# Row maxima of the first two heads of a group on 32-row tiles of the TensorE array

## The reference, cut to what matters

```python
# layer 0: 16 heads of 4 columns, layer 1: 16 heads of 8 columns; 512 queries, 512 keys, 2 sequences
scores = einsum('bhsk,bhtk->bhst', Q, K) / sqrt(hd)
attn   = softmax(scores, axis=-1)        # needs the largest score of every query row
out    = einsum('bhst,bhtv->bhsv', attn, V)
```

## Time and profile before

| | |
|---|---|
| time, median of 3 runs | 538.16 us (537.77 to 544.53) |
| time of the profiled execution | 538.86 us |
| its span | 537.1 us |
| granted TensorE clock, mean | 0.976 |
| PE busy | 481.1 us (90%) |
| DVE busy | 315.2 us (59%) |
| ACT busy | 278.7 us (52%) |
| main loop of layer 0 | about 137 to 250 us |
| main loop of layer 1 | about 327 to 449 us |

### The profile page before, as it was taken

The page is one execution under the profiler, slowest core; times in us unless marked ns, Lnnn a source line. Parts: engine busy times, 40 slices in busy tenths (PEclk is TensorE's granted clock), DMA queues, the critical chain, the costliest instruction groups (busy, mean ns, idle before and its releaser), DMA issues.

```text
span 537.1 us, 7612 instructions
## 1 busy us (share of the span) xinstructions
PE 481.1 (90%) x2782; PEld 313.7 (58%) x2782; DVE 315.2 (59%) x826; ACT 278.7 (52%) x414; POOL 136.3 (25%) x136
## 2 busy tenths in 40 slices
PE   5899799999889999999999988989999988879970
PEld 4678678887433443434997864334443434769970
DVE  4654544566787878764263576877888762402223
ACT  6635343553455666778454653556665664106540
POOL 5765713331631011210100000101111005422561
PEclk9999899999999999999999997999999999989995
DMA  8970200000610000020000000000000004430003
GB/s 315 316 237 2 77 2 0 1 0 2 237 77 0 1 2 0 1 79 0 2 1 0 1 2 1 1 0 1 0 1 2 0 1 160 189 106 2 19 18 121
DMA packets 12868, 26.57 MB, mean 49 GB/s; under 512 B 1293, under 2 KB 10120, under 8 KB 11808
## 3 DMA queue, kind: packets, MB, share of 16 engines
q1 hardware_dynamic: 11392, 22.91, 12.5%
q0 software_dynamic: 1440, 3.18, 1.9%
HBM read 22.11 MB, written 5.26 MB: 51 GB/s over the span
## 4 chain that ended last, share of the span: by engine, by line
PE 71%; DVE 15%; ACT 5%; DMA 3%; issue 3%; POOL 1%; SPq 0%; POOLq 0%; DVEq 0%; ACTq 0%
PE PS L436 13%; PE PS L469 10%; DVE mx L1154 7%; PE PS L614 5%; PE PS L691 5%; PE PS L580 5%; PE PS L582 5%; PE PS L581 5%; PE PS L722 4%; PE PS L731 3%; PE PS L454 3%; PE PS L342 3%; PE PS L421 2%; DVE work L1053 1%; ACT wc_late L855 1%
## 5 line engine op out<-in xcount | busy, mean ns | idle before, releaser
L1154 DVE TENSOR_REDUCE mx<-PS 128x1 f32<-128x512 f32 x256 | 164.5, 685 | 37.4 <-PE PS L436 36.7
L855 ACT ACTIVATE wc_late<-PS 128x1024 f32<-128x1024 f32 x128 | 123.7, 1023 | 57.8 <-PE PS L454 57.7
L436 PE MATMUL PS<-Kp,Qs 128*128 128x512 f32 x256 | 103.8, 466 | 11.7 <-DVE mx L1154 6.2
L436 PEld LDWEIGHTS PS<-Kp,Qs 128*128 128x128 f32 x256 | 43.1, 190 | 85.0 <-DVE mx L1154 45.9
L469 PE MATMUL PS<-wc_late,v_c 128*16 128x512 f32 x512 | 67.4, 598 | 1.2 <-ACT wc_late L855 1.2
L1439 POOL CAST Kp<-Ks 32x512 fp32r<-32x512 f32 x40 | 24.3, 607 | 131.9 <-ACT Ks L834 130.0
L580 PE MATMUL PS<-wc_late_r 128*128 128x512 f32 x96 | 42.2, 440 | 0.5 <-POOL work_r L1401 0.5
L1053 DVE TENSOR_SCALAR work<-PS,early 128x512 f32<-128x512 f32 x32 | 22.5, 746 | 25.8 <-PE PS L582 25.8
L955 ACT ACTIVATE work<-PS,late 128x160 f32<-128x160 f32 x64 | 20.0, 395 | 33.7 <-PE PS L722 33.7
L454 PE MATMUL PS<-Qm,Kp 32*128 32x512 f32 x256 | 35.1, 504 | 2.5 <-ACT wc_late L855 1.4
L1067 DVE SCALAR_TENSOR_TENSOR x_tok<-PS,cw,x_tok 128x128 f32<-128x128 f32 x64 | 18.0, 344 | 30.9 <-PE PS L691 30.9
(11 more groups left out here) (244 smaller groups left out, 745.9 us busy)
## 6 DMA issues: line engine op xcount, KB each, us to landing
wa<-wa_dram SPq DMA_DIRECT2D x8, 512.0 KB, 8.9
wa<-wc_dram SPq DMA_DIRECT2D x2, 2048.0 KB, 9.7
wc_late<-wc_dram SPq DMA_DIRECT2D x2, 2048.0 KB, 10.6
wb<-wb_dram SPq DMA_DIRECT2D x1, 2048.0 KB, 15.5
sel<-sel_dram POOLq DMA_DIRECT2D x2, 1024.0 KB, 5.4
late<-late_dram SPq DMA_DIRECT2D x1, 1572.0 KB, 14.0
packed_rows<-ao SPq DMA_DIRECT2D x1, 1290.0 KB, 21.6
wb<-packed_rows SPq DMA_DIRECT2D x5, 258.0 KB, 4.8
```

The costliest lines, as they stand in the source:

```text
L436: filled(mm(p, Qs[:, G % 3, qt * P:(qt + 1) * P], Kp[:, G % 3, j, :], start=True, stop=True), (L, "max", G, qt, j))
L855: A(E4[:, 2 * (i % 2) + jp, :, :], p, ACT.Exp, scale=float(HD[L]) ** -0.5).then_inc(taken[f"s{jp}"], 1)
L1154: V.reduce_max(mx[:, G % 2, qt, j:j + 1], p, AX.X).then_inc(taken[filled_at[key][0]], 1)
```

## The change

The products of half 0 (heads 0 and 1) are limited to the strip of their head: 32 rows of `Qs` and `Kp` at rows 0 to 31 for head 0 and 32 to 63 for head 1, on the tile of the array that begins at that row. The rows left out held zeros in `Kp`, so that the result is the same. Half 1 (heads 2 and 3) keeps all 128 rows. No instruction is added, removed or moved on any engine; waits and banks are as before.

```diff
                     for j in (2 * half, 2 * half + 1):
                         p = claim((L, "max", G, qt, j), slots[j % 2])
-                        filled(mm(p, Qs[:, G % 3, qt * P:(qt + 1) * P], Kp[:, G % 3, j, :], start=True, stop=True),
-                               (L, "max", G, qt, j))
+                        r = slice(SL * j, SL * (j + 1)) if half == 0 else slice(0, P)
+                        filled(mm(p, Qs[r, G % 3, qt * P:(qt + 1) * P], Kp[r, G % 3, j, :], start=True, stop=True,
+                                  tile_position=(r.start, 0)), (L, "max", G, qt, j))
```

## The result

The changed kernel takes 554.0 us (median of 4 runs, 553.35 to 556.54) where the kernel before takes 538.65 in the same comparison: ratio 1.027, with an interval of 1.0189 to 1.035. The forecast was 540.5 us with a range of 533.5 to 547, so the time lies outside of it, 7.0 us above its upper end.

A forecast was written before the change was run, and what follows sets the result against it. It took a chain of waits alternating between DVE and PE, not busy time, as the bound. Terms +3.8 - 2.9 + 1.4 = +2.3 us on 538.86 gave 541.2, less 0.7 for the median: 540.5 us, range 533.5 to 547.

The forecast's parts named there:

- The round of 3.74 us: One main-loop step's chain of waits, alternating DVE reductions and PE (head 1, job, values, head 2): 3.74 us.
- The 34 us of busy time: PE busy time for 128 maxima products that would come off if they cost as little as scores: 34 us.
- rival 2: PE's busy time really comes off, a third to all of 34 us: 504 to 527 us, chance 0.05.
- (a): 21 pairs with head 1 held by a reduction, whole-array job behind: the passage falls on the path, +3.8 us.
- (c): 18 main-loop pairs not held by a reduction, 13 counted: overlap gains 0.22 us each, -2.9 us.
- (b): 12 pairs with head 1 held by a reduction, values right behind: passage was there before and stays, 0 us.
- (d): 10 pairs between the experts: one more passage at either side, 0.17 us each for eight, +1.4 us.
- Forecast 0.54: Chance 0.54 given to the whole kernel's time falling between 538.5 and 543.5 us.
- rival 3: PE's clock falls in more stretches, first in layer 0's first steps: about 542.5 us; beyond 2%, chance 0.06.
- one more stretch of two thin steps: Price set for a clock fall in thin steps, first at 138 to 146 us: +1 to +2 us.
- the four full steps that decide: Four full steps at half clock, some 2 us each, would make the kernel slower: 549 us and above, up to 560.

The follow-up runs named there:

- e13: Kernel before, with only the stack issued ahead of the pair of half 0, in steps 1, 5, 9 and so on: 542.7 us, ratio 0.9971.
- e11: Kernel before, whole-array maxima, with all jobs of place 0 (stack, turn, maxT) issued ahead of the pair of half 0: 546.5 us, ratio 1.0107.
- the streams: Three runs of separate kernels without the computation, only PE products in sections of 40 steps paced by VectorE; the clock was read per section.
- the first streams: Computation-free kernel varying rows per product: two whole-array products a step kept clock 1.00, two on 32 or 64 rows fell to 0.50.
- e5: Kernel before with only head 0 of each quarter on its 32-row tile, head 1 on the whole array: 547.8 us, ratio 1.0119.
- e6: Kernel before with all four heads on 32-row tiles, 256 tile products: 579.6 us, 568.8 to 588.4.
- the last streams: Computation-free kernel repeating passage tests in another order: four passages a step gave clock 0.50, two gave 1.00; forty steps took 111 against 43 us.
- e12: The order of e11 with heads 0 and 1 on 32-row tiles as in the change: 562.5 us, ratio 1.0371 to the kernel before.
- e1: Kernel before with the change's tiles only for groups 3 to 7, 40 of the 64 pairs: 541.5 us, ratio 1.0048.
- the second streams: Computation-free kernel mixing whole-array and tile products: only the section alternating whole array and single tiles fell to clock 0.50, the others stayed at 1.00.

## Why the prediction was wrong, point by point

**What bounds the kernel: right.** The round of 3.74 us through two reductions, head 1, the job and values stands: e13 and e11 shortened it by the job. The 34 us of busy time were not there to be had; rival 2 fell.

**(a) held pairs with a job behind: right in mechanism and size.** Forecast 1.10 us from head 1 to values, measured 1.09. In layer 0's steps 6 to 29, nine such steps grew by 0.13 to 0.20 us, 1.6 us together, and one step of (c) gave back 0.14.

**(b) held pairs with values behind: right.** Steps 8, 12, 16 and 20 take 2.82 us in both traces.

**(c) pairs not held: mis-sized.** Forecast -2.9 us, measured about -0.9: five steps at full clock got shorter, by 0.14 to 0.20 us each (step 10 of layer 1 from 4.26 to 4.07). Elsewhere the next wait took the gain, as the turn's bank did at 186.17 us. I had excluded the waits that the trace of before shows, and not the ones close behind them.

**(d) pairs between the experts: right in layer 0, too high in layer 1.** Layer 0's five pairs lost 0.8 us (0.17 each was forecast): the first product of an output stood 0.87 us earlier than in the trace before at 99.6 us, and 0.08 earlier at 135.5. Layer 1's four pairs up to 328 us lost 0.16 us together (the outputs stood 10.49 us later than before at 316 us and 10.65 later at 332); the clock fell behind them.

**The step that failed: "Forecast 0.54" at an unchanged clock, with rival 3 at 0.06.** Its mechanism is what happened, at the place that I had named first (138 to 146 us), and its price for a full step was near (1.6 us measured, "some 2 us" said). But I priced it as one more stretch of two thin steps, +1 to +2 us, and gave the four full steps that decide as a far case. The sum itself put the term at nothing, since the loops ran at 1.00 with PE at 93% busy, and I took that as a margin. It is none: the trace has some 36 us more at half clock (26 to 62), and 12.2 us were lost in the parts with such stretches ahead of step 30 of layer 1. The terms at full clock came out near the sum: +2.3 us forecast, and 2.0 in steps 6 to 29 of layer 0 and 3 to 29 of layer 1, and 0.8 between layer 0's experts.

In the streams a section with products under way in 102.7 of 102.7 us had the lower clock. The Trainium skill, page "TensorE: Matmul & The Clock Gate", section "What's actually happening", says that the gate is set by how busy the PE has been; busy in the profile's sense it cannot be, by these runs: they show that two products on 128 rows held the clock where two on 32 or 64 did not, and that four passages a step lost it with the same products, at more than twice this kernel's density of passages. The change leaves rows idle and adds few passages or none in the loops, so the idle rows are what the streams and this kernel share.

**How the two shares stand.** Shown: idle rows alone lower the clock (the first streams; e5 and e6 fit); passages do when they are dense (the last streams); the loss of the change goes with the clock (12.2 of 14.1 us in the trace ahead of step 30 of layer 1; e12 against e11, 16.0 us) and falls away where the steps are dense (e1). Not shown: that passages have a share in this kernel's falls. Open stays why heads 2 and 3 on tiles, with as many idle rows and no fewer passages, cost just 0.5%; this speaks against idle rows as the whole cause. Open too is why a fall came in the last steps of layer 0's loop, where both kernels issue the same: it may be that a later start alone moved it there. Some runs of the kernel before show a mean clock of 0.967 to 0.971 (541.9 to 546.9 us), which one to three such stretches more would make; no trace of such a run is at hand.

## What to carry to other kernels

A 32-row tile of the array is worth its passages only if several tiles run at once and stay together; a pair between two whole-array jobs pays two passages for one overlap (0.8 us for layer 0's five pairs), and where VectorE frees the banks one by one there is no overlap to win. Before thinning the work of TensorE, look for the steps in which it already waits: there the clock at 1.00 has no margin that the profile shows, and the first fall here (141.1 to 151.4 us) made two steps 3.9 us longer, more than the 2.9 us that I had forecast as the gain. Price the fall first, then the edit.

## What the runs showed of the hardware that I had not expected

- Products whose moving operand is zero in 96 of 128 rows hold the clock as full ones do (1.00 in sections 2 and 3 of the first streams); leaving these rows out of the tile loses it (0.50 in section 4), at the same two products a step. By that the "wasted" rows of zeros are what kept the array at 2.4 GHz in this kernel's thin steps; this is carried over from the streams and not shown in the kernel itself.
- Four 32-row tiles at once with one whole-array product a step stayed at 1.00 (26.5 us, last section of the second streams); two tiles at once, alone, went to 0.50.
- Four passages a step, in place of two and a pair at once, cost 1.7 - 1.09 = 0.6 us at full clock and, with the fall that they bring, 2.89 - 1.09 = 1.8 us.
